# A sparse expert layer told expert by expert: one list of tokens per expert instead of one slot per token and choice

## The reference, cut to what matters

```python
NUM_EXPERTS, NUM_KEPT, TOP_K, HIDDEN, INTER, CAP = 128, 48, 8, 256, 96, 96
old_to_new = -1 except old_to_new[2*i] = i for i < 48        # the experts that are kept
h = layernorm(x)                                             # T x 256
# router logits over the 128 experts, those not kept at -1e30; the top 8 of a token;
# softmax over the 8 gives its weights
# an expert takes its first CAP = 96 tokens, in order; later ones are dropped
y_e = (silu(h_e @ Wg_e) * (h_e @ Wu_e)) @ Wd_e               # 96 x 256 per expert
x  += sum over a token's experts of weight * its row of y_e
```

## Time and profile before

| | us |
|---|---|
| median of 3 runs | 4484.63 (4478.69 to 4495.13) |
| the profiled execution: time, span | 4505.4, 4503.6 |
| PE, DVE, ACT, POOL busy | 3543.0, 2730.2, 1614.0, 1555.6 |
| mean PEclk | 0.896 |

### The profile page before, as it was taken

How to read it: one execution, slowest core, us unless ns; L and a number is a source line. 1 busy time by engine, 2 the same in 40 slices (tenths; PEclk the granted TensorE clock), 3 DMA queues, 4 the chain that set the end, 5 groups by cost and what they waited for, 6 DMA issues and landing times. The chain is left out here.

```text
span 4503.6 us, 58245 instructions
## 1 busy us (share of the span) xinstructions
PE 3543.0 (79%) x17574; PEld 2742.3 (61%) x17574; DVE 2730.2 (61%) x7933; ACT 1614.0 (36%) x4118; POOL 1555.6 (35%) x2243
## 2 busy tenths in 40 slices
PE   6999993589577999999999999847999999940320
PEld 4677662455366888888888888735655655530320
DVE  4666652532257888888888888545666666652123
ACT  2434441123234545555555555313444444410100
POOL 0000000058515555555555555501111111117357
PEclk9999995589778999999999999978999999965665
DMA  2000004135411111111111111110000000021340
GB/s 69 0 0 0 0 0 106 63 61 84 85 30 34 29 38 24 38 24 38 28 37 41 24 38 24 19 56 1 0 0 0 0 0 0 0 91 39 100 116 13
DMA packets 225351, 152.21 MB, mean 34 GB/s; under 512 B 125496, under 2 KB 211702, under 8 KB 224096
## 3 DMA queue, kind: packets, MB, share of 16 engines
q1 hardware_dynamic: 192880, 113.99, 9.8%
q0 software_dynamic: 27456, 30.91, 3.7%
q10 hardware_dynamic: 4800, 4.72, 0.3%
HBM read 117.41 MB, written 56.11 MB: 39 GB/s over the span
## 5 line engine op out<-in xcount | busy, mean ns | idle before, releaser
L1869 DVE SCALAR_TENSOR_TENSOR dl_y<-ps,dl_taps,dl_y 128x255 f32<-128x255 f32 (+2 forms) x1536 | 653.0, 475 | 130.6 <-ACT dl_y L1765 126.4
L1600 PE MATMUL ps<-xnT,dl_wkqv 128*128 128x256 f32 x2048 | 544.8, 392 | 29.0 <-DVE dl_lp L1912 23.3
L1600 PEld LDWEIGHTS ps<-xnT,dl_wkqv 128*128 128x128 f32 x2048 | 370.4, 194 | 81.2 <-issue 38.2
L366 POOL TENSOR_TENSOR at_rs<-at_ss,mhalf 128x15 f32<-128x15 f32 x32 | 125.5, 3921 | 745.8 <-DVE at_ss L553 745.8
L1523 POOL TENSOR_TENSOR dl_rn<-dl_n,mhalf 128x4 f32<-128x4 f32 x128 | 173.3, 1354 | 553.0 <-DVE dl_n L1885 553.0
L452 PE MATMUL ps<-at_shared,at_v 128*128 128x256 f32 (+2 forms) x1280 | 315.7, 380 | 4.6 <-ACT at_shared L676 0.2
L1765 ACT ACTIVATE dl_y<-ps,dl_taps 128x256 f32<-128x256 f32 x512 | 260.2, 560 | 106.2 <-PE ps L1600 106.2
L428 PE MATMUL ps<-at_kT,at_qT 128*128 128x320 f32 (+2 forms) x1024 | 271.2, 397 | 2.8 <-ACT at_kT L658 2.8
L1541 POOL TENSOR_TENSOR dl_inv_u<-dl_inv_u,dl_inv_tmp 64x30 f32<-64x30 f32 (+14 forms) x480 | 259.0, 540 | 37.6
L452 PEld LDWEIGHTS ps<-at_shared,at_v 128*128 128x128 f32 (+1 forms) x1280 | 211.1, 190 | 89.3 <-issue 64.0
L392 PE MATMUL ps<-at_wq,at_xb 128*128 (+1 forms) x512 | 246.1, 614 | 4.5 <-POOL at_xb L360 2.4
(11 more groups left out here) (332 smaller groups left out, 7944.7 us busy)
## 6 DMA issues: line engine op xcount, KB each, us to landing
dl_grow<-decay_rows SPq DMA_DIRECT2D x128, 128.0 KB, 3.0
sp_wgu<-in_w1gu SPq DMA_DIRECT2D x12, 768.0 KB, 10.5
dl_wkqv<-in_w1kqv SPq DMA_DIRECT2D x16, 512.0 KB, 4.9
delta_diag<-dl_lp SPq DMA_DIRECT2D x512, 8.0 KB, 1.5
dl_diag<-delta_diag_tt SPq DMA_DIRECT2D x512, 8.0 KB, 1.7
moe_wgu<-in_w0gu SPq DMA_DIRECT2D x16, 448.0 KB, 10.4
slot_rows<-sp_zero SPq DMA_DIRECT2D x4, 1152.0 KB, 8.1
sp_wd<-in_w1d SPq DMA_DIRECT2D x12, 384.0 KB, 12.0
```

The lines of the kernel that those rows point to most:

```text
L1600: last = nc.tensor.matmul(bank(h, m // 2, (m % 2) * S, (m % 2 + 1) * S), wkqv[h][:, c, m * P:(m + 1) * P], k.xnT[:, c, u.seq * S:(u.seq + ...
L1869: last = nc.vector.scalar_tensor_tensor(y[h][:, m, back:S], bank(h, m // 2, (m % 2) * S, (m % 2 + 1) * S - back), taps[h][:, m, KC - 1 - b ...
```

## The change: what it does

`SparseWeights(k, st)` is a new block ahead of the last layernorm: SP loads the constants, stores x into one table and zeros into the other, and loads the first 16 experts' weights; after it come the layernorm and one single block `sparse_experts(k, s)`.

The router's weights are first cut to the 48 kept experts by a product with a one-hot matrix. The eight largest logits are found as before, but no index of them: the mask alone is kept. Counting uses a scan over tiles in bf16. Then DVE makes the key `128*(expert+1) + place` of each chosen pair, `max` takes the eight keys of a token apart, and for each tile one-hot matrices of place (`lanes`) and expert (`owner`, which ACT scales by a code of the token) are multiplied on PE in bf16, so that column e of a 96 x 48 matrix is the list of expert e's tokens. POOL then fetches the 96 rows of an expert with one DMA from a table that also holds the weights, and adds the 96 weighted results to one of two tables with one accumulating DMA: 48 of each. The two tables are read back in four parts, on the queues of SP and ACT, added on DVE and stored.

In the diff below, in this order: the new block (SP), POOL's scatters of before and its fetches and adds of now, PE's products that place the tokens and its order over the experts, DVE's one-hot matrices, and the call in `build`.

```diff
+        with nc.Block() as block:
+            @block.sync
+            def _(sp):
+                for to, name in ((self.iota, "c_iota"), (self.pidx, "c_pidx"), (self.trib, "c_trib"),
+                                 (self.onesb, "c_onesb"), (self.gateT, "w1rT")):
+                    sp.dma_start(to[:, :], ins[name]).then_inc(self.loaded, 16)
...
+                sp.dma_start(self.acc[0][0:T].rearrange("(t p) d -> p t d", p=P), k.x[:, :, :]).then_inc(self.stored, 16)
+                sp.wait_ge(self.zeroed, 1)
+                sp.dma_start(self.acc[1][0:T].rearrange("(t p) d -> p t d", p=P),
+                             self.zero[:, 0:D].unsqueeze(1).to_broadcast([P, NT, D])).then_inc(self.stored, 16)
...
+                for q in range(WB):
+                    self.load(sp, k, q)
...
-                        for j in range(TOPK1):
-                            nc.gpsimd.indirect_dma_start(
-                                out=xrows, out_offset=bass.IndirectOffsetOnAxis(slot_i[:, i, j:j + 1], axis=0),
-                                in_=k.xn_rows[:, i, :], in_offset=None, bounds_check=SLOTS - 1,
-                                oob_is_err=False).then_inc(scattered, 16)
...
+                def fetch(e):
+                    if e >= RX:
+                        pool.wait_ge(turned, e - RX + 1)
+                        pool.wait_ge(y_ready, e - RX + 1)
+                    nc.gpsimd.indirect_dma_start(
+                        out=xs[e % RX][:, :], out_offset=None, in_=s.xtab,
+                        in_offset=bass.IndirectOffsetOnAxis(index[:, e:e + 1], axis=0),
+                        bounds_check=ROWS - 1, oob_is_err=True).then_inc(fetched[e % RX], 16)
+
+                def add(e):
+                    pool.wait_ge(y_ready, e + 1)
+                    if e >= 2:
+                        pool.wait_ge(added[e % 2], 16 * (e // 2))
+                    nc.gpsimd.indirect_dma_start(
+                        out=s.acc[e % 2], out_offset=bass.IndirectOffsetOnAxis(index[:, e:e + 1], axis=0),
+                        in_=y[e % RY][:, :], in_offset=None, bounds_check=ROWS - 1, oob_is_err=True,
+                        compute_op=ALU.add).then_inc(added[e % 2], 16)
+
+                pool.wait_ge(index_ready, 1)
+                pool.wait_ge(s.stored, 96)
+                for e in range(AHEAD):
+                    fetch(e)
+                for e in range(EK):
+                    if e + AHEAD < EK:
+                        fetch(e + AHEAD)
+                    add(e)
...
+                for i in range(NT):
+                    pe.wait_ge(coded, i + 1)
+                    for j in range(TOPK1):
+                        last = nc.tensor.matmul(k.ps[0][0:CAP, 2, 0:EK], lanes[i % RO][:, j, :], owner_code[i % RO][:, j, :],
+                                                start=i == 0 and j == 0, stop=i == NT - 1 and j == TOPK1 - 1)
+                    last.then_inc(placed, 1)
...
+                turn(0)
+                for e in range(EK + 1):
+                    if e < EK:
+                        up(e)
+                    if e + 1 < EK:
+                        turn(e + 1)
+                    if e >= 1:
+                        down(e - 1)
...
+                for i in range(NT):
+                    if i >= RO:
+                        dve.wait_ge(placed, i - RO + 1)
+                    nc.vector.tensor_tensor(lanes[i % RO][:, :, :], iotab[:, 1:CAP + 1].unsqueeze(1).to_broadcast([P, 8, CAP]),
+                                            lob[:, i, :].unsqueeze(2).to_broadcast([P, 8, CAP]), ALU.is_equal)
+                    nc.vector.tensor_tensor(owner[i % RO][:, :, :], iotab[:, 0:EK].unsqueeze(1).to_broadcast([P, 8, EK]),
+                                            hib[:, i, :].unsqueeze(2).to_broadcast([P, 8, EK]), ALU.is_equal).then_inc(lanes_made, 1)
...
-            k.xn_rows = k.sb("xn_rows", [P, NT, D], F32, st)
-            layernorm(k, k.xn_rows)
-            sparse_experts(k)
+            s = SparseWeights(k, st)
+            layernorm(k, s.rows[:, :, 0:D])
+            sparse_experts(k, s)
```

More of the change, by code:

```diff
@@ L25 @@
 U32 = mybir.dt.uint32
+U16 = mybir.dt.uint16
 ALU = mybir.AluOpType
@@ new lines, in _ @@
+                last.then_inc(logits_ready, 1)
+                pe.wait_ge(summed, 1)
+                for h in range(2):
+                    o = k.ps[1][:, h, 0:HT * EK]
+                    nc.tensor.matmul(o, s.trib[:, :], m[:, h * HT:(h + 1) * HT, :].rearrange("p t e -> p (t e)"), start=True, stop=False)
+                    last = nc.tensor.matmul(o, s.onesb[:, :],
+                                            scan[4][:, PAD - 1 + h * HT:PAD - 1 + (h + 1) * HT, :].rearrange("p t e -> p (t e)"),
+                                            start=False, stop=True)
@@ new lines, in _ @@
+                for e in range(EK + 1):
+                    if e < EK:
+                        silu(e)
+                    if e >= 1:
+                        weigh(e - 1)
+                for q in range(2):
+                    act.wait_ge(added[q], 16 * (EK // 2))
+                for c in range(PARTS):
+                    act.dma_start(s.rows[:, NP * c:NP * c + NP, 0:D],
+                                  s.acc[1][P * NP * c:P * NP * (c + 1)].rearrange("(t p) d -> p t d", p=P)).then_inc(back[c], 16)
@@ new lines, in _ @@
+                dve.wait_ge(logits_ready, 1)
+                for h in range(2):
+                    last = nc.vector.tensor_tensor(lg[:, h * HT:(h + 1) * HT, :],
+                                                   k.ps[0][:, h, 0:HT * EK].rearrange("p (t e) -> p t e", e=EK),
+                                                   neg[:, :].unsqueeze(1).to_broadcast([P, HT, EK]), ALU.add)
+                ch.link(last)
+                for i in range(NT):
+                    last = nc.vector.max(best[:, i, :], lg[:, i, :])
@@ new lines, in _ @@
+                for h in range(2):
+                    t = slice(h * HT, (h + 1) * HT)
+                    before = k.ps[1][:, h, 0:HT * EK].rearrange("p (t e) -> p t e", e=EK)
+                    nc.vector.scalar_tensor_tensor(kept[:, t, :], before, CAP - 0.5, m[:, t, :], ALU.is_lt, ALU.mult)
+                    last = nc.vector.tensor_tensor(key[:, t, :], before, ebase[:, :].unsqueeze(1).to_broadcast([P, HT, EK]), ALU.add)
+                ch.link(last)
+                ch.link(nc.vector.tensor_tensor(key[:, :, :], key[:, :, :], kept[:, :, :], ALU.mult))
@@ new lines, in _ @@
+                for i in range(NT):
+                    last = nc.vector.max(keys[:, i, :], key[:, i, :])
+                ch.link(last)
+                ch.link(nc.vector.tensor_scalar(hi[:, :, :], keys[:, :, :], 1.0 / P, -0.5 + 0.5 / P, ALU.mult, ALU.add))
+                ch.link(nc.vector.tensor_scalar(hi[:, :, :], hi[:, :, :], MAGIC, MAGIC, ALU.add, ALU.subtract))
+                nc.vector.tensor_copy(hib[:, :, :], hi[:, :, :])
+                ch.link(nc.vector.scalar_tensor_tensor(lob[:, :, :], hi[:, :, :], -float(P), keys[:, :, :], ALU.mult, ALU.add))
@@ L2381 @@
+                keep_x(0)
+                for e in range(EK):
+                    if e + 1 < EK:
+                        keep_x(e + 1)
+                    gate_up(e)
+                for c in range(PARTS):
+                    dve.wait_ge(back[c], 32)
+                    xt = k.x[:, NP * c:NP * c + NP, :]
+                    nc.vector.tensor_tensor(xt, xt, s.rows[:, NP * c:NP * c + NP, 0:D], ALU.add).then_inc(joined, 1)
 class SelfRope:
```

475 lines of the change are left out of this document (222 added, 253 removed).

## The result

| | before | after |
|---|---|---|
| median, us | 4489.88 of 4 runs (4478.69 to 4495.35) | 4272.66 of 4 runs (4269.09 to 4276.32) |
| profiled execution: time, span, us | 4505.4, 4503.6 | 4269.09, 4267.3 |
| from the attention's end to the end of the span, us | 525.3 | 298.7 |

The ratio is 0.9521 (95% interval 0.9507 to 0.9535): faster by 4.8%, 217 us by the medians. The time is 2.7 us above the forecast range and 41 above the forecast.

A forecast was written before the change was run, and what follows sets the result against it. POOL's 128 indirect DMAs each way were taken to bound the last layer's scatters and gathers (338 of 367 us). Terms summed to 272.7 us for 525.6, 252.9 less: 4232 us, own range 4208 to 4256, with rivals 4203 to 4270.

The forecast's parts named there:

- the loop's term: Last layer's expert loop: 41 pairs of fetch and add on POOL take 110.7 us, bounds 106.6 to 133.7.
- 2.70 near the lower end: Expert loop on POOL: a fetch and add of 96 rows take 2.70 us, against 3.26 with 128 rows.
- The difference between gather and accumulate, 0.53 us: Expert loop's DMAs of the same count: the 0.53 us between gather and accumulating DMA looks like a price per row.
- this wait: Expert loop: an add's wait for the add two before on its table, 2.3 us, stays hidden under a 2.6 us pair.
- Rival 1: Expert loop: 96 rows cost what 128 do, or half-clock PE bounds at 3.1 to 3.3 us; 4255 us, chance 0.16.
- Rival 2: Expert loop: DVE and POOL block each other, a period of some 5 us, 94 us more; 4326 us, chance 0.06.
- Rival 3: New block's edge ahead of the layernorm costs nothing, SP's issue being covered by the queue: 30 us less, 4202, chance 0.07.
- rival 4: Expert loop doesn't overlap, adds holding up fetches on POOL's queue; slower than before from 8.1 us an expert; 4770 us, chance 0.03.
- The block: New block ahead of the layernorm: the layernorm waits for SP to issue all its loads, 32 us, bounds 27 to 36.
- Logits: Routing: 64 records as before, bound by loading 128 x 128 weights on PE, taken at 12 us, near the cold clock.
- `lanes` and `owner`: Routing: DVE's one-hot comparisons, 1152 elements a tile, take 1.33 us, 21.3 us over 16 tiles.
- 1.16 ns per element: Routing: DVE's assumed rate, with some 0.1 us per instruction, from L1201's 1.47 us for 1264 elements.

The follow-up runs named there:

- e5_plain: The changed kernel with the adds' accumulation dropped, so they are plain scatters of the same 96 rows: 4250.52 us (1 run).
- e4_rows: The changed kernel with experts fetching and adding only their first 96, 64, 32 or 16 tokens, by turns of two experts: 4270.27 us (1 run).
- e1_noload: The changed kernel without the eight weight loads inside the expert loop; experts 16 to 47 use the first 16's weights: 4261.99 us, ratio to before 0.9493.
- e7_tables: The changed kernel with four tables of sums in turn in place of two, only the first two read back: 4263.24 us, ratio to before 0.9492.
- e3_hidden: The changed kernel with table stores and first four pairs of weight loads moved from the block ahead of the layernorm into the routing: 4250.02 us, ratio to before 0.9464.
- e8_stores: The changed kernel with only the first weight loads moved behind the layernorm, stores and constants left in the block: 4254.51 us, ratio to before 0.9443.
- e6_pack: The changed kernel with both one-hot matrices laid out with the eight choices innermost: 4279.91 us, ratio to before 0.9521.

## Why the prediction was right and wrong

**What bounds the kernel.** Right. The POOL stages went, the direction and nine tenths of the size with them: 226.6 us of 525.3 in this layer, where 252.9 were forecast.

**The step that failed** is the loop's term, "41 pairs: 110.7 us", by two mis-sized parts of it. First its price: "with 96 rows the work can shrink by a quarter at most ... so I take 2.70 near the lower end". The difference between gather and accumulate, 0.53 us, was read as a price per row; e5_plain shows it to be the price of accumulating, and e4_rows that rows hardly count. The price was 3.04, near the 3.26 of the earlier trace rows, and 13.9 us of the miss. The earlier trace rows could have warned: all their DMAs have 128 rows, so they say nothing of a price per row, and a plain scatter took 0.979 us and the gathers 1.038 and 1.061, while only the one that accumulates took 1.586. Second, "that this wait doesn't bind inside the loop follows: 2.3 is under 2.6". The 2.3 came from the end of the first layer, where nothing else moved; beside a load of 1.15 MB a landing takes up to 7.7 us and the wait binds, 12.9 us. e1_noload and e7_tables show it from either end of the mechanism. The pairs forecast at 2.70 took 3.35 on average.

**The rivals.** Rival 1's first half (96 rows cost what 128 do) was nearly the case: 3.04 is 61% of the way from 2.70 to 3.26. Its second half, PE's half clock, wasn't: e1_noload ran at 0.66 without a stall. No rival had the add's wait for its table in it. Rival 2 didn't occur: no DVE row stands in POOL's waits. Rival 3 fell with e3_hidden and e8_stores, rival 4 with a period of 3.4 us where it needed 8.1.

**The terms that held.** The block: 31.9 for 32, and SP's issue is its cause, as e3_hidden and e8_stores show by taking it apart. That it hit to a tenth is luck: 32 was taken between bounds of 27 and 36. Logits at half clock, 13.9 us where 12 was taken, are most of the routing's 2.9 us. `lanes` and `owner` held, 1.34 us a tile for 1.33, and e6_pack shows that this price does hang on the innermost step. (The 1.16 ns per element are all of L1201's 1.47 us; the 0.1 us per instruction named beside them was in them already, and this term rightly left it out.) What was over in these terms and what was under nearly cancels: 0.8 us.

**What is left.** In the trace the layer explains 226.6 us; the profiled executions differ by 236.3 and the medians by 217.2. The rest comes from layers that the change doesn't touch, whose end varies by 15 us over these profiles; no experiment separates it further. Of the 41 us between forecast and median 26 are this layer's. About 5 are the median of before, which rose from 4484.6 to 4489.9 with a fourth run, and the other 10 or so are the untouched layers. That the median ended 2.7 us above the range and not just inside it is less than they vary; the loop's 26.8 us are not.

## What to carry to other kernels

Between 16 and 128 rows of 1 KB, price an indirect DMA by the piece and not by the row (1.31 to 1.59 us of POOL when it accumulates, 0.94 to 1.06 for a gather): fewer of them pays, smaller ones hardly do. A wait that is free when nothing else moves must be priced at the landing time beside the largest transfer that shares the engines; if it then binds, cut that transfer or put more work between the two uses. And a block of loads costs the next block all of its issue: put the loads where a stage already waits for something else.

## What the runs showed that was not expected

- POOL's time for an indirect DMA: fetch 1.00, 1.01, 0.98, 0.94 us and accumulating add 1.44, 1.43, 1.33, 1.31 us for 96, 64, 32, 16 rows; a plain scatter of 96 rows 0.95 (rows of e4_rows and e5_plain).
- An accumulating DMA of 96 rows landed in 3.4 us without weight loads beside it (e1_noload, median) and in up to 7.7 beside a pair of them; a plain scatter goes from 2.4 (median) to 8.3 (e5_plain).
- PE's eight bf16 products of 96 x 48 took 0.83 us a tile with weights at a step of 1 and 1.42 at a step of 8, at a PEclk of 0.50 both times; ACT's copy of 384 bf16 elements per partition took 0.615 and 0.985 us at input steps of 1 and 8.
